# An attention and mixture-of-experts block: the products with V made by halves of the queries, with a mixed V brought by DMA

## The reference, cut to what matters

```python
h = layernorm(x) * (1 + ca) + sa
q, k, v = h @ Wq.T, h @ Wk.T, h @ Wv.T        # 16 query heads, 4 key/value heads, D = 64
scores = 30 * tanh((q . k) / 8 / 30)
mask = (j <= i) & (j > i - 128)               # causal, a window of 128 keys
o = softmax(where(mask, scores, -1e30)) . v   # each k/v head serves 4 query heads
x = x + ga * (o @ Wo.T)
h = layernorm(x) * (1 + cb) + sb
# 8 experts, top 1, capacity 512: token -> relu(h @ W1[e] + b1[e]) @ W2[e] + b2[e], times its gate
x = x + gb * moe(h)
```

## Time and profile before

| | us |
|---|---|
| median of 3 timed runs | 507.95 |
| lowest and highest | 506.22, 508.55 |
| the profiled execution, its own time | 503.43 |
| its span | 501.7 |

### The profile page before, as it was taken

How to read it: one execution, slowest core, us unless ns; L and a number is a source line. 1 busy time by engine, 2 the same in 40 slices (tenths; PEclk the granted TensorE clock), 3 DMA queues, 4 the chain that set the end, 5 groups by cost and what they waited for, 6 DMA issues and landing times. The chain is left out here.

```text
span 501.7 us, 11629 instructions
## 1 busy us (share of the span) xinstructions
PE 448.1 (89%) x3976; PEld 273.8 (55%) x3976; DVE 345.7 (69%) x1061; ACT 295.8 (59%) x505; POOL 285.9 (57%) x398
## 2 busy tenths in 40 slices
PE   2899999999999999999999999999998951599991
PEld 1655555555545555465555545646563431499981
DVE  4387586857887878588787876887768775145552
ACT  3677565667574847676656576766665532355530
POOL 3245464665656656756565658565757574035564
PEclk9999999999999999999999999999999995599997
DMA  8984000000000000000000000000000013991110
GB/s 244 370 281 169 5 7 7 23 23 24 23 23 24 24 23 24 23 23 25 23 23 24 24 23 22 24 24 24 23 23 24 23 62 95 323 359 61 37 44 30
DMA packets 27474, 33.56 MB, mean 67 GB/s; under 512 B 2477, under 2 KB 23788, under 8 KB 27417
## 3 DMA queue, kind: packets, MB, share of 16 engines
q1 hardware_dynamic: 24344, 24.54, 15.1%
q0 software_dynamic: 3072, 8.28, 4.6%
HBM read 15.88 MB, written 17.31 MB: 66 GB/s over the span
## 5 line engine op out<-in xcount | busy, mean ns | idle before, releaser
L1175 POOL TENSOR_SCALAR_AFFINE_SELECT PM<-PR 128x1024 f32<-128x1024 f32 x64 | 69.9, 1092 | 56.6 <-ACT PR L645 56.5
L818 DVE COPY_PREDICATED own<-before,turns 64x512 f32<-64x512 uint32 x112 | 77.9, 696 | 32.0 <-PE own L403 29.7
L639 ACT ACTIVATE PR<-own 128x1024 f32<-128x1024 f32 x64 | 65.6, 1024 | 45.3 <-DVE own L818 37.7
L1183 POOL TENSOR_TENSOR OL<-O,OH 128x512 fp32r<-128x512 f32 x64 | 81.3, 1281 | 5.4 <-ACT OH L651 5.3
L645 ACT ACTIVATE PR<-PR 128x1024 f32<-128x1024 f32 x64 | 67.7, 1058 | 1.0
L394 PE MATMUL own<-Q,K 64*64 64x512 f32 x112 | 59.8, 614 | 2.2 <-ACT PR L639 1.4
L419 PE MATMUL turns<-PR,V 128*32 128x512 f32 x448 | 59.4, 602 | 0.0
L419 PE MATMUL turns<-PM,VD 128*32 128x512 f32 x448 | 58.3, 592 | 0.0
L1211 POOL DMA_INDIRECT sorted_rows<-PAY,slot_i x32 | 33.8, 1056 | 41.1 <-issue 40.2
L399 PE MATMUL own<-Q,K 64*64 64x512 f32 x112 | 57.0, 589 | 0.0
L848 DVE TENSOR_TENSOR O<-turns,R 128x512 f32<-128x512 f32 x64 | 44.1, 688 | 17.5 <-PE turns L419 16.8
(11 more groups left out here) (202 smaller groups left out, 1333.9 us busy)
## 6 DMA issues: line engine op xcount, KB each, us to landing
sorted_rows<-PAY SPq DMA_DIRECT2D x1, 6400.0 KB, 22.9
x_sb<-x_dram SPq DMA_DIRECT2D x4, 512.0 KB, 7.9
w_stage<-w_dram SPq DMA_DIRECT2D x1, 2048.0 KB, 10.9
out_dram<-PAY SPq DMA_DIRECT2D x32, 64.0 KB, 1.7
x_sb<-sorted_rows SPq DMA_DIRECT2D x2, 800.0 KB, 9.2
Q<-sorted_rows SPq DMA_DIRECT2D x2, 800.0 KB, 9.1
PR<-sorted_rows SPq DMA_DIRECT2D x2, 800.0 KB, 9.1
O<-w_dram SPq DMA_DIRECT2D x4, 256.0 KB, 7.9
```

The costliest lines, as they stand in the source:

```text
L639: act.activation(pr, own[:, :, :].rearrange("p a n -> p (a n)"), ACT.Tanh, scale=SCORE_SCALE).then_inc(tanhed, 1)
L818: dve.copy_predicated(own[mine, :, :].rearrange("p a (r n) -> p (a r) n", n=P)[:, :, mine], before[mine, mine].bitcast(U32).unsqueeze(1).t ...
L1175: pool.affine_select(out=PM[:, u % P_RING, :].rearrange("p (r n) -> p r n", n=P), in_=PR[:, u % P_RING, :].rearrange("p (r n) -> p r n", n ...
L1183: pool.tensor_tensor(OL[:, t % 2, x, :], O[:, t % 2, x, :], OH[:, t % 2, x, :].bitcast(F32), ALU.subtract).then_inc(ol_done, 1)
```

## The change

- `attend(t)` makes both x of a tile in one call. It takes two neighbouring banks, and they now stand for halves of the queries (c = 0: queries 0 to 63, c = 1: queries 64 to 127) instead of for x.
- For c = 0, V(t - 1) is used as before for all 128 key positions. For c = 1 the V of the first 64 positions would always be that of tile t, so a mixed V is used: VM has V(t) in partitions 0 to 63 and V(t - 1) in 64 to 127. Two DMAs from SP for each tile that isn't first (`mix_v`) bring it, 64 partitions by 1 KB each.
- The correction with VD and PM is then needed only on the two 64x64 diagonal blocks: for c = 0 with key positions 0 to 63, for c = 1 with positions 64 to 127. Each is a matmul with 64 rows, 32 weight columns and 256 moving columns, at `tile_position=(64 * c, 32 * g)`.
- `scale(t, c)` works on a half of the queries; O, OH and OL are ordered by c, x, head. `out_project` reads them in runs of 64.
- `pv_half` is gone: both halves of a tile are told done together. SP's stores of x1 and the new DMAs stand in a written order.
- HOME and the orders on all engines are new. The tasks in them are the same, but for attend. In the new list of ScalarE `keep_y`, `keep_h2`, `high_o(e, 0)` and `gate_row` stand between the second exp of an odd tile and the tanh of the next score call; on VectorE the splits of Wo come before `scale(0, ...)`; on GpSimd both `low_o` of a tile stand together.

```diff
-K_RING, Q_RING, V_RING, VD_RING, P_RING, PAY_RING = 3, 2, 6, 4, 4, 4
+K_RING, Q_RING, V_RING, VD_RING, VM_RING, P_RING, PAY_RING = 3, 2, 6, 4, 4, 4, 4
...
+    ("before", 0, 0): 2, ("before", 0, 1): 3, ("before", 1, 0): 4, ("before", 1, 1): 1,
+    ("count", 0): 5, ("count", 1): 3,
+    ("h2", 0): 3, ("h2", 1): 0,
+    ("k",): 0,
+    ("logits", 0): 2, ("logits", 1): 4,
+    ("pv", 0): 4, ("pv", 1): 0,
+    ("q", 0): 2, ("q", 1): 3, ("q", 2): 4, ("q", 3): 3,
+    ("sums", 0): 5, ("sums", 1): 2,
+    ("v",): 1,
+    ("wo",): 1,
+    ("x",): 1,
+    ("y", 0): 5, ("y", 1): 0,
...
+def mixes(t):
+
+    return t // BATCH_TILES + 1 if t % VM_RING == 0 else t // VM_RING + 1
...
-            for t in range(TILES):
+
+            def mix_v(t):
+
+                if first(t):
+                    return
+                sp.wait_ge(v_kept, t // 2 + 1)
+                if t >= VM_RING:
+                    sp.wait_ge(pv_done, t - VM_RING + 1)
+                for half, tile in enumerate((t, t - 1)):
+                    sp.dma_start(VM[HALVES[half], t % VM_RING, :], V[HALVES[half], tile % V_RING, :]).then_inc(mixed_in[t % VM_RING], 16)
+
+            def store_x(t):
...
+            for e in range(8, TILES + 16, 2):
+                if is_tile(e - 10):
+                    mix_v(e - 10)
+                if is_tile(e - 15):
+                    store_x(e - 15)
+                if is_tile(e - 14):
+                    store_x(e - 14)
+                if is_tile(e - 9):
+                    mix_v(e - 9)
...
+            def attend(t):
...
+                n, ps = take_two("pv", t)
+
+                def out_of(c, x, g):
+                    return ps[32 * g:32 * g + 32, c, x * 2 * P:(x + 1) * 2 * P].rearrange("p (r n) -> p r n", n=HALF)
+
+                def probabilities(p, rows, g, c):
+                    return p[rows, (2 * t + g // 2) % P_RING, g % 2 * REP * P:(g % 2 + 1) * REP * P].rearrange(
+                        "p (r n) -> p r n", n=P)[:, :, HALVES[c]]
...
+                    pe.wait_ge(mixed_in[t % VM_RING], 32 * mixes(t))
+                for x in range(2):
+                    for c in range(2):
+                        v = V[:, t % V_RING, :] if first(t) else VM[:, t % VM_RING, :] if c else V[:, (t - 1) % V_RING, :]
+                        for g in range(KV):
+                            d = slice(g * D + 32 * x, g * D + 32 * x + 32)
+                            last = pe.matmul(out_of(c, x, g), v[:, d], probabilities(PM if first(t) else PR, slice(0, P), g, c),
+                                             start=True, stop=first(t), tile_position=(0, 32 * g))
+                    if first(t):
+                        continue
                     for g in range(KV):
...
+                        d = slice(g * D + 32 * x, g * D + 32 * x + 32)
+                        for c in range(2):
+                            last = pe.matmul(out_of(c, x, g), VD[HALVES[c], t % VD_RING, d], probabilities(PM, HALVES[c], g, c),
+                                             start=False, stop=True, tile_position=(HALF * c, 32 * g))
+                last.then_inc(pv_done, 1)
+                freed[n] = scaled, 2 * t + 1
+                freed[n + 1] = scaled, 2 * t + 2
...
-                    h, r = divmod(i, REP)
-                    oh, ol = (o[:, :, h, r * P:(r + 1) * P] for o in (OH, OL))
+                    oh, ol = (o[:, :, :, i * HALF:(i + 1) * HALF] for o in (OH, OL))
...
-                dve.tensor_tensor(O[:, t % 2, x, :], bank["pv", t, x], R[:, :], ALU.mult).then_inc(scaled, 1)
+                inverse = R[:, :].rearrange("p (r n) -> p r n", n=P)[:, :, HALVES[c]].unsqueeze(1).to_broadcast([P, 2, REP, HALF])
+                dve.tensor_tensor(O[:, t % 2, c, :].rearrange("p (x r n) -> p x r n", x=2, n=HALF),
+                                  bank["pv", t][:, c, :].rearrange("p (x r n) -> p x r n", x=2, n=HALF), inverse, ALU.mult).then_inc(scaled, 1)
```

More of the change, by code:

```diff
@@ L188, in build @@
         w2_in = [sem(f"w2_in{n}") for n in range(EXPERTS)]
+        mixed_in = [sem(f"mixed_in{n}") for n in range(VM_RING)]
         final_out = [sem(f"final_out{n}") for n in range(2)]
@@ L404, in score @@
                 freed[n] = freed[n + 1] = merged, merges(t, h, 1)
[L406 to L417, removed]
-                    for g in range(KV):
[L419 to L423, removed]
+            def attend(t):
[5 more added lines that the diff above has]
+                        "p (r n) -> p r n", n=P)[:, :, HALVES[c]]
+                pe.wait_ge(masked, 2 * t + 2)
+                if t % 2 == 0:
+                    pe.wait_ge(v_kept, t // 2 + 1)
+                if not first(t):
+                    pe.wait_ge(exped, 2 * t + 2)
+                    pe.wait_ge(vd_done, later_tiles(t) + 1)
+                    pe.wait_ge(mixed_in[t % VM_RING], 32 * mixes(t))
[8 more added lines that the diff above has]
+                        continue
+                    for g in range(KV):
+                        d = slice(g * D + 32 * x, g * D + 32 * x + 32)
[5 more added lines that the diff above has]
+                freed[n + 1] = scaled, 2 * t + 2
@@ L425, in sums @@
             def sums(t):
                 n, ps = take("sums", t)
-                pe.wait_ge(masked if first(t) else exped, 2 * t + 2)
+                if first(t):
+                    pe.wait_ge(masked, 2 * t + 2)
+                else:
+                    pe.wait_ge(exped, 2 * t + 2)
                 for g in range(KV):
@@ L488, in program_pe @@
             pe.wait_ge(consts, CONSTS)
[L492 to L527, removed]
-                if is_tile(e - 6):
[L529 to L542, removed]
@@ new lines, in program_pe @@
+            for e in range(-4, TILES + 8, 2):
+                if is_tile(e):
+                    project_q(e // 2, 2)
+                if is_tile(e - 2):
+                    sums(e - 2)
+                if is_tile(e - 7):
+                    count(e - 7)
+                if is_tile(e - 1):
+                    score(e - 1, 1)
+                if is_tile(e - 2):
+                    attend(e - 2)
+                if is_tile(e - 4):
+                    out_project(e // 2 - 2)
+                if is_tile(e - 6):
+                    count(e - 6)
+                if is_tile(e):
+                    score(e, 0)
+                if is_tile(e - 5):
+                    turn_h2(e - 5)
+                if is_tile(e):
+                    project_v(e // 2)
+                if is_tile(e - 4):
+                    turn_y(e - 4)
+                if is_tile(e - 5):
+                    score_experts(e - 5)
+                if is_tile(e + 2):
+                    project_k(e // 2 + 1)
+                if is_tile(e - 1):
+                    sums(e - 1)
+                if is_tile(e):
+                    score(e, 1)
+                if is_tile(e - 1):
+                    attend(e - 1)
+                if is_tile(e + 2):
+                    project_q(e // 2 + 1, 1)
+                if is_tile(e + 1):
+                    score(e + 1, 0)
+                if is_tile(e - 4):
+                    turn_h2(e - 4)
+                if is_tile(e + 2):
+                    project_q(e // 2 + 1, 0)
+                if is_tile(e - 3):
+                    turn_y(e - 3)
+                if is_tile(e + 4):
+                    turn_x(e // 2 + 2)
+                if is_tile(e + 2):
+                    project_q(e // 2 + 1, 3)
+                if is_tile(e - 4):
+                    score_experts(e - 4)
@@ L699, in program_act @@
                     split_high(SPLIT_O1)
                     split_high(SPLIT_O0)
[L701 to L710, removed]
-                if is_tile(e + 10):
-                    weigh(e + 10, 1)
-                    expose(e + 10, 1)
@@ L742, in program_act @@
[L742 to L746 removed]
+                if is_tile(e - 14):
+                    keep_v(e // 2 - 7)
+                if is_tile(e - 12):
+                    keep_k(e // 2 - 6)
+                if is_tile(e - 16):
+                    high_o(e - 16, 1)
+                if is_tile(e - 14):
+                    weigh(e - 14, 1)
+                    expose(e - 14, 0)
```

420 lines of the change are left out of this document (204 added, 216 removed).

## The result

| | runs | median, us | lowest, highest |
|---|---|---|---|
| before | 20 | 507.51 | 505.85, 508.94 |
| after | 20 | 510.03 | 506.47, 511.89 |

The ratio of after to before is 1.0042, 95% interval 1.0026 to 1.0059: a little slower, where 490 us was forecast and 473 to 506 given as the range. The profiled executions span 501.7 and 508.8 us.

The account below looks back on a forecast made before the run. TensorE's own instruction list was taken to bound the loop. 503.4 - 13.8 (attend) - 8 - 3 (order) + 5.8 + 1.5 (mixed V) + 1 (early tanh waits) + 1 (tail) = 487.9, plus 2 for unprofiled runs: 490 us, range 473 to 506.

Parts of the forecast that it names:

- Does the rest keep up?: Loop, other engines: banks free in time, 5.6 us of slack a pair in the score-tanh chain, VectorE 82% busy.
- Attend: columns: Attend on TensorE: eight correction parts overlap, 0.85 us instead of 1.71, removing 23.9 us over 28 tiles.
- Rival (c): Correction in attend: eight parts don't run at once; four at a time gives 514 us, further out 533; chance 0.12.
- Attend: changes of shape: Within a tile's attend: three changes between 128-row and 64-row parts, 0.12 us each, cost 10 us in all.
- The new order: TensorE's list in the loop: fewer stretches of one shape save 8 us, shorter waits of `turn_h2` 3 us.
- The mixed V: Tile 1's attend: `mix_v(1)` queues behind the w1 load, stalling TensorE 5.8 us, then 1.5 for a slower clock.
- The tail: After the last attend: scales, copies and subtractions all follow the whole tile before `out_project`, 4.5 us instead of 3.6, +1 us.
- Rival (b): Loop: TensorE starts to wait, waits on VectorE or ScalarE above 15 us; 500 to 506 us, chance 0.16.

Follow-up runs that it names:

- the short `low_o`: Kernel after with GpSimd's low_o cut from 512 to 16 columns from tile 2 on: 487.31 us, 0.9596 of the kernel before.
- both edits and two changes: Kernel after with normalise1 moved, w1 loaded at step 20, and two changes of shape a tile instead of three: 480.40 us, repeated at 476.77 us.

## Why the prediction was wrong

Forecast 490, in a range from 473 to 506; measured 510.0 against 507.5. The step that failed is "Does the rest keep up?": it found 5.6 us of slack a pair and priced VectorE's waits at nothing, and the place of one VectorE instruction cost 19 us. Point by point:

- **Attend: columns.** Right. Eight parts at once, 0.853 us of columns less a tile. Rival (c), whose band of 508 and above the time fell into, is out: a correction takes 0.59 us, not 0.85.
- **Attend: changes of shape.** Right in kind, a little low: 0.12 was taken and 0.16 to 0.18 measured. The tile went from 3.58 to 3.19, 0.39 instead of 0.49, 10.9 us instead of 13.8. The price of 0.12 was taken from the row of entering a tiled shape (0.09); the rows of leaving one (0.15 to 0.17) were nearer.
- **The new order.** 8 and 3 us were taken; the old products in the new order with `normalise1` moved give 13. How that divides between shapes and waits wasn't measured.
- **The mixed V.** Right: 5.8 and 1.5 us forecast, 6.4 and 1.8 measured, by the mechanism named, and gone with w1 moved. The wait differs from one execution to another with the landing of w1: 3.9 to 6.4 us in three profiles.
- **The tail.** Low. From the last correction to the experts' first transposes it is 27.8 us (405.6 to 433.4) against 25.1 (404.0 to 429.1), +2.7 for +1 forecast. The wait before `out_project` is 4.3 instead of 3.6 us, and the clock is at 1.2 GHz behind it (granted 0.50 from 411 to 415 us): the matmuls are 0.21 us apart instead of 0.12, 24 times, 2.3 us. It is no accident of one execution: from the first to the last of the 24 it takes 2.70 us in the kernel before and 4.15 to 5.05 in every profile with the new lists but the one with the short `low_o` (2.78). Rows of the kernel after:

```profile
409.86 0.55 PE L495 MATMUL turns<-OH,WoH 128*128 128x256 f32 x1 [2.35 <-POOL OL L1232]
410.21 0.41 PE L496 MATMUL turns<-OL,WoH 128*128 128x256 f32 x1
410.42 0.41 PE L497 MATMUL turns<-OH,WoL 128*128 128x256 f32 x1
```

  The experts, whose code is unchanged, took 75.4 us in this profile against 72.6. Over the profiles of the study this part lies between 71.5 and 75.9, and for one and the same kernel (both edits and two changes) at 75.9 and 72.7; so single executions spread by 3 us here, and whether the medians hold any of it isn't shown.
- **"Does the rest keep up?"** This step failed. It walked the lists with the durations of the kernel before as if they belonged to the instructions alone. That of `normalise1` depends on what GpSimd does beside it. The sign was in the trace of the kernel before, in a line that wasn't among the rows; after the count stand least, median and greatest ns:

```profile
L800 DVE TENSOR_SCALAR XN<-x_sb,mv,rstd x32: 334/827/1302, 7.6 to 337.7; 128x128 f32<-128x128 f32 x32
```

  One instruction on one shape, between 0.33 and 1.30 us. The prediction took VectorE's sum of 282 us over, where it became 304 in the same stretch (it had said that VectorE's busy time would stay within 2%; over the span it grew by 6%), and the 5.6 us of slack a pair were found without asking how long the entries of the new list would take where they now stand. The new lists put `normalise1(e + 16)` right behind `normalise2`, which waits for GpSimd's `rstd2_of`; so in 11 pairs running it begins as GpSimd goes on to the scatter and both `low_o`, and the merges of the tile's second score call come right after it.
- **Rival (b)** is what happened, at 500 to 506 with a chance of 0.16, with the engine right and the cause missing. Its sign came true: TensorE's waits for VectorE and ScalarE in the stretch are 10.7 + 4.6 + 0.9 + 0.8 = 17.0 us, above the 15 that it named. Its price was a guess at lost slack, 14 us; the move of one task gives 19, and the time lies above its band.

By the sum: forecast 490, + 19 for `normalise1` = 509, + 3 for the dearer changes, + 2 for the tail, - 2 for the order = 512, against 510 measured. With `normalise1` alone moved the changed kernel is at 0.9672 of the kernel before, 490.9 us of 507.5, so next to the forecast. That it comes so near is in part luck: the changes and the tail were too cheap, and the order made up for about half of it.

## What to carry to other kernels

Before a list is reordered, look at the least and the greatest duration of each group, not only at its mean: an instruction whose time varies on one shape may be waiting inside itself for another engine, as `normalise1` did for GpSimd, and its time will be another at another place. When a change shortens the engine that bounds the loop, look at the places where a short instruction of a second engine meets long ones of a third. And what is new in a DMA queue can be late where the queue is full; here that was at the start, once, and it cost twice: the wait and the clock after it.

## What the runs showed of the hardware

- A VectorE `tensor_scalar` of 128x128 float32 from SBUF to SBUF takes 0.33 us alone and up to 3.9 us beside GpSimd's `tensor_tensor` and what follows it without a gap. With its result in PSUM it takes 0.41 us, beside a `low_o` too (the one at 70.21). An indirect DMA on GpSimd doesn't hold the first form (0.34).
- Eight float32 matmuls (two passes each) of 64 rows, 32 weight columns and 256 moving columns run side by side in 0.59 us with the change of shape, 0.43 of it columns; sixteen, in two rounds, in 1.03.
- A change between parts of 128 and of 64 rows costs TensorE 0.16 to 0.18 us in these attends.
- A transfer of 64 KB issued by SP behind a load of 2 MB landed up to 11.1 us after its issue, where the median of the 56 is 2.0; with the load moved away the slowest took 3.5.
